# Modulation pieces and the first half's y moved inside a selective scan, and the norm, router and base matmuls after it taken by halves

## The reference

```python
mod = (_silu(L0_c) @ L0_wmod).reshape(1, 6, 1, -1)        # sa, ca, ga, sb, cb, gb; the same again with L1_wmod
h = _layernorm(x) * (1 + ca) + sa
# scan: xp = h @ x_proj_w.T -> dt_in, B, C;  dt = softplus(dt_in @ dt_proj_w.T + b)
#   state = exp(dt * A) * state + dt * B * h     per token, 512 channels x 16 states
#   y = sum over states of state * C  + D * h
x = x + ga * y
h = _layernorm(x) * (1 + cb) + sb
# base_out = h @ base_W.T + b;  logits = h @ router_W.T;  softmax, top 8 of 15, expert weights w
# lora = ((h @ A) * w) @ B * 2
x = x + gb * (base_out + lora)
# layer 1: modulation, layer norm, attention, modulation, layer norm, feed-forward
```

## Time and profile before

| what | value |
|---|---|
| median of 3 runs | 991.18 us (986.23 to 992.69) |
| the profiled execution, time | 988.8 us |
| its span, first to last instruction | 987.0 us |
| PE busy | 877.2 us (89%) |
| DVE busy | 749.6 us (76%) |
| ACT busy | 439.2 us (45%) |
| POOL busy | 264.5 us (27%) |
| mean granted TensorE clock | 0.957 of full speed |

### The profile page before, as it was taken

The page is one execution under the profiler, slowest core; times in us unless marked ns, Lnnn a source line. Parts: engine busy times, 40 slices in busy tenths (PEclk is TensorE's granted clock), DMA queues, the critical chain, the costliest instruction groups (busy, mean ns, idle before and its releaser), DMA issues.

```text
span 987.0 us, 12212 instructions
## 1 busy us (share of the span) xinstructions
PE 877.2 (89%) x4378; PEld 423.7 (43%) x4384; DVE 749.6 (76%) x1191; ACT 439.2 (45%) x822; POOL 264.5 (27%) x213
## 2 busy tenths in 40 slices
PE   3678868887776899989999999999999999999996
PEld 3224424443224544434455555555444444444442
DVE  6579999888899565637887788787524699876776
ACT  1637575645552102110066666666752465533200
POOL 1027789887894300005000000000000144200000
PEclk8769899999997999997999999999999999999998
DMA  9100060300002202451022211220006000000001
GB/s 353 65 1 0 1 255 1 128 0 1 0 0 72 100 0 89 135 181 38 15 69 74 74 37 40 73 75 2 2 1 224 5 0 1 0 1 0 12 33 43
DMA packets 29382, 54.35 MB, mean 55 GB/s; under 512 B 8021, under 2 KB 14805, under 8 KB 28041
## 3 DMA queue, kind: packets, MB, share of 16 engines
q1 hardware_dynamic: 29320, 53.57, 16.2%
HBM read 44.96 MB, written 8.39 MB: 54 GB/s over the span
## 4 chain that ended last, share of the span: by engine, by line
PE 58%; DVE 5%; SPq 3%; issue 3%; ACT 1%; DMA 0%; POOL 0%; DVEq 0%; POOLq 0%
PE ps L1075 15%; PE ps L940 8%; PE ps L922 6%; PE ps L1086 6%; PE ps L904 4%; PE ps L909 3%; PE ps L996 3%; PE ps L976 3%; SPq L302 2%; PE ps L857 2%; PE ps L962 2%; PE ps L925 1%; PE ps L907 1%; PE ps L851 1%; PE ps L725 1%
## 5 line engine op out<-in xcount | busy, mean ns | idle before, releaser
L678 ACT ACTIVATE prob<-ps 128x512 f32<-128x512 f32 x288 | 161.8, 599 | 138.6 <-PE ps L925 105.9
L458 POOL TENSOR_TENSOR hC<-hs,C_sb 128x512 f32<-128x512 f32 x128 | 163.0, 1284 | 70.1 <-DVE hs L1240 59.5
L832 PE MATMUL ps<-hC,identf 128*128 128x512 f32 x256 | 137.1, 644 | 35.6 <-POOL hC L458 33.5
L1354 DVE TENSOR_REDUCE mrow<-ps 128x4 f32<-128x512 f32 x160 | 103.7, 687 | 24.1 <-PE ps L907 15.8
L922 PE MATMUL ps<-stack 123*128 123x512 bf16 (+3 forms) x384 | 113.7, 327 | 0.2
L414 POOL TENSOR_TENSOR rstd<-veps,mhalf 128x4 f32<-128x4 f32 x8 | 8.4, 1052 | 381.4 <-DVE veps L1113 381.4
L612 ACT ACTIVATE ps<-dtT,nA 128x512 f32<-128x512 f32 x128 | 88.3, 691 | 42.2 <-DVE hs L1240 42.0
L1357 DVE TENSOR_REDUCE mrow<-ps 128x1 f32<-128x512 f32 x128 | 82.2, 685 | 25.1 <-PE ps L909 25.1
L832 PEld LDWEIGHTS ps<-hC,identf 128*128 128x128 f32 x256 | 45.3, 197 | 109.5 <-POOL hC L458 90.9
L1218 DVE TENSOR_TENSOR dBx<-uT,ps 128x512 f32<-128x512 f32 x112 | 74.9, 669 | 21.0 <-ACT B_sb L590 14.4
L940 PE MATMUL ps<-prob,V 128*32 128x512 f32 (+3 forms) x768 | 81.6, 498 | 0.7 <-ACT prob L678 0.7
(11 more groups left out here) (192 smaller groups left out, 1328.0 us busy)
## 6 DMA issues: line engine op xcount, KB each, us to landing
stack<-parts_dram SPq DMA_DIRECT2D x192, 64.0 KB
wmod<-in_wmod SPq DMA_DIRECT2D x4, 1536.0 KB, 11.2
parts_dram<-qkp SPq DMA_DIRECT2D x48, 128.0 KB, 1.8
wmod<-in_wmod SPq DMA_DIRECT2D x4, 1024.0 KB, 9.9
wattn<-in_wattn SPq DMA_DIRECT2D x1, 3072.0 KB, 10.3
wg<-in_wg SPq DMA_DIRECT2D x1, 2752.0 KB, 12.2
wu<-in_wu SPq DMA_DIRECT2D x1, 2752.0 KB, 9.5
wd<-in_wd SPq DMA_DIRECT2D x1, 2560.0 KB, 11.5
```

What stands on the lines that cost most here:

```text
L458: pool.tensor_tensor(hC[:, c, :], hs[:, c, :], C_sb[:, m % 2, :], ALU.mult).then_inc(S["hc_done"], 1)
L678: A_(prob[:, u % 4, j, :], ps[:, 3 + F % 3, :], ACT.Exp).then_inc(S["exp_done"], 1)
L832: mm(ps[:, c, :], identf[:], hC[:, c, :], start=False, stop=(s == NS - 1), skip_group_check=True).then_inc(S["sum_done"], 1)
L1354: v.reduce_max(mrow[:, kb, :, i], ps[:, bank, :].rearrange("p (j c) -> p j c", c=P), AX) \
```

## The change

1. **Pieces inside the step.** From step 16 on a piece stands on PE after the second of the step's four sums (`c == 2`) and no longer ahead of `broadcast(m + 1)`. ACT's copy of it goes to the next step. The piece now waits for C's copy of the next step (`c_evac` at `m + 2`).
2. **Rows in halves.** The 512-column rows are cut in two pieces of 256 columns: steps 7 and 8 for layer 0, 21 to 24 for layer 1. The column pieces of layer 1 stand in steps 12 to 15 and 17 to 20. SP's load of layer 1's wmod follows the piece of step 8.
3. **The first half's y.** The sixteen turning matmuls and the copies to uT leave step 16; `y_start` waits only for ACT's copy of the bank (`ym`). Four new pieces of kind "y" in steps 25 to 28 put a token tile of x into C_BANK by a matmul with the identity, add the four turned chunks on top, and ACT copies the sum to x_tok. The four DVE additions after the scan are gone.
4. **Halves after the scan.** DVE norms the first four tiles before it adds y to the last four. PE turns the first four, makes their router product, turns the last four, makes base_out(0), and then the router product of the last four; base_out(4) stands between hw's transposes and `lora_out`. The PSUM banks are dealt anew by `AR_BANK` and `F0_BANK`. SP's bias loads wait for the last turn (`yt`), no longer for x (`x0`).

```diff
+        for i_ in range(6):
+            SLOTS[1 + i_] = ("cols", 0, 2 + i_ // 2, i_ % 2 * 2)
+        for i_ in range(2):
+            SLOTS[7 + i_] = ("row", 0, 5, i_)
+        for i_, m_ in enumerate((12, 13, 14, 15, 17, 18, 19, 20)):
+            SLOTS[m_] = ("cols", 1, (0, 1, 3, 4)[i_ // 2], i_ % 2 * 2)
+        for i_ in range(4):
+            SLOTS[21 + i_] = ("row", 1, (2, 5)[i_ // 2], i_ % 2)
+            SLOTS[25 + i_] = ("y", None, None, i_)
...
+        AR_BANK = (0, 1, 4, 5)
+        F0_BANK = (2, 3, 6, 7, 4, 5, 6, 7)
...
-            sp.wait_ge(S["x0"], NT)
+            sp.wait_ge(S["yt"], NT)
...
+                if kind == "y":
+                    act.wait_ge(S["yt"], part + 1)
+                    A_(x_tok[:, part, :], ps[:, C_BANK, :], ACT.Copy).then_inc(S["x0"], 1)
+                    return
...
-                    if m == NS and c >= 2:
-                        for t in (2 * c - 4, 2 * c - 3):
-                            act.wait_ge(S["yt"], t + 1)
-                            A_(uT[:, t, half(0)], ps[:, t, :], ACT.Copy).then_inc(S["yb"], 1)
-                    if c == 2 and m in SLOTS:
-                        modulation(m)
+                    if c == 2 and m < NS and m in SLOTS:
+                        slot_out(m)
+                    if c == 2 and m > NS and m - 1 in SLOTS and m - 1 >= NS:
+                        slot_out(m - 1)
...
+            def slot(m):
+                kind, layer, j, part = SLOTS[m]
+                pe.wait_ge(S["c_evac"], m + 1 if m < NS else m + 2)
+                if kind == "y":
+                    pe.wait_ge(S["ym"], DC)
+                    pe.wait_ge(S["dg"], 2 * DC)
+                    mm(ps[:, C_BANK, :], identf[:], x_tok[:, part, :], start=True, stop=False, skip_group_check=True)
+                    for c in range(DC):
+                        ins = mm(ps[:, C_BANK, c * P:(c + 1) * P], dtT[:, c, tile(part)], dgA[:, c, :], start=False,
+                                 stop=(c == DC - 1), skip_group_check=True)
+                    ins.then_inc(S["yt"], 1)
+                    return
...
                 if h:
-                    pe.wait_ge(S["yb"], c + 1)
+                    pe.wait_ge(S["ym"], c + 1)
                 mm(ps[:, c, :], dgD[:, c, :], hT[:, c, half(h)], start=True, stop=False, skip_group_check=True)
...
-                    if c == 0 and m in SLOTS:
-                        modulation(m)
+                    if c == 0 and m in SLOTS and m < NS or c == 2 and m in SLOTS and m >= NS:
+                        slot(m)
...
                     broadcast(NS + 1)
-                    pe.wait_ge(S["dg"], 2 * DC)
-                    for c in range(DC):
-                        turn(0, c)
                     for c in range(DC):
                         y_start(1, c)
...
+            ln_transpose(1, 0)
+            pe.wait_ge(S["in_lf"], 48)
+            router(0)
+            ln_transpose(1, 1)
+            base_out(0)
+            router(1)
+            for t in range(1, 4):
                 base_out(t)
             pe.wait_ge(S["hw_done"], 1)
             for t in range(NT):
                 pe.transpose(ps[:, t // 4, (t % 4) * P:(t % 4 + 1) * P], hw[:, t, :], identf[:]) \
                     .then_inc(S["hw_tr"], 1)
+            base_out(4)
             pe.wait_ge(S["hw_evac"], 2)
-            for t in range(4):
+            for t in range(5):
                 lora_out(t)
...
             for t in range(4):
-                v.wait_ge(S["yb"], t + 1)
-                tt(x_tok[:, t, :], x_tok[:, t, :], uT[:, t, half(0)], ALU.add).then_inc(S["x0"], 1)
-            for t in range(4):
                 v.wait_ge(S["x0"], t + 1)
                 ln_stats((t,))
             ln_var(0)
-            for t in range(4):
-                v.wait_ge(S["yt"], 4 + t + 1)
-                tt(x_tok[:, 4 + t, :], x_tok[:, 4 + t, :], ps[:, 4 + t, :], ALU.add).then_inc(S["x0"], 1)
+            ln_norm(1, 0)
+            for t in range(4, NT):
+                v.wait_ge(S["yt"], t + 1)
+                tt(x_tok[:, t, :], x_tok[:, t, :], ps[:, t, :], ALU.add).then_inc(S["x0"], 1)
             for t in range(4, NT):
                 v.wait_ge(S["x0"], t + 1)
                 ln_stats((t,))
             ln_var(1)
-            ln_norm(1, 0)
             ln_norm(1, 1)
```

More of the change, by code:

```diff
@@ L829, in _ @@
                         pe.wait_ge(S["c_evac"], N_ALL)
-                        turn(1, 0)
+                        turn(0)
                     pe.wait_ge(S["hc_done"], m * DC + c + 1)
@@ L867, in _ @@
                     .then_inc(S["hw_tr"], 1)
+            base_out(4)
             pe.wait_ge(S["hw_evac"], 2)
-            for t in range(4):
+            for t in range(5):
                 lora_out(t)
-            for t in range(4, NT):
-                pe.wait_ge(S["f0_y"], t - 3)
+            for t in range(5, NT):
+                if t >= 6:
+                    pe.wait_ge(S["f0_y"], t - 3)
                 base_out(t)
@@ L1336, in gated @@
                                 ln_norm(norm, 0)
-            gated("f0_mm", "f0_y", "x1", "x1pre", lambda t: 4 + t % 4, gb0, norm=2)
+            gated("f0_mm", "f0_y", "x1", "x1pre", lambda t: F0_BANK[t], gb0, norm=2)
             ln_norm(2, 1, (0, 2))
```

85 lines of the change are left out of this document (41 added, 44 removed).

## The result

The changed kernel takes 964.66 us (median of 4 runs, 961.34 to 965.73), the kernel before on the same chip 991.71 (4 runs, 986.23 to 992.69): the ratio is 0.973, 95% interval 0.969 to 0.976. The forecast was 963.5, the range 957 to 972. The profiled execution after took 964.11 us, its span is 962.3 (before 987.0) and its mean granted clock 0.968 (before 0.957). So the spans differ by 24.7 us, against 25.3 forecast. The medians differ by 27.1 us: the forecast was taken off the profiled execution of before, which lies 2.9 us under this median. The total agrees better than its parts.

The account below looks back on a forecast made before the run. DVE was taken to set the pace in the scan's second half, waiting 14.4 us for B_sb, with PE leading from about 350 us. 13.7 + 1.9 + 9.7 = 25.3 us off the profiled 988.8 gave 963.5, range 957 to 972.

Parts of the forecast that it names:

- The pieces behind two sums: Scan's second half: twelve pieces fit on PE between second and third sum, counted at nothing, 0.2 us at the tightest place.
- 0.7 us left at step 18: Scan, step 18: the broadcast comes about 1.2 us late against 0.5 us of slack, so 0.7 us of waiting stays.
- the sign that I had named: Scan's second half in the profile after: steps 17 to 28 longer than 6.7 us would show the prediction wrong.
- The second half's term, 13.7: Scan's second half: DVE's 14.4 us of waits for B_sb fall to 0.7, gaining 13.7 us; bounds 2.3 and 14.4.
- slower: Rival: PE at half clock in the scan's second half, twelve pieces at 3.12 us each, 1000.2 us; chance 0.02.
- The row of step 7, 1.9: Scan's first half: cutting the row removes DVE's waits of 1.08 + 0.82 us, gaining 1.9 us; bounds 0.9 and 1.9.
- After the scan, 9.7: Behind the scan: hw's transposes 9.0 us earlier plus 0.74 us of PE standing covered, 9.7 us; bounds 8.7 and 11.5.
- The upper bound of 11.5: Behind the scan: the largest gain, with the fast router value and the transposes at half their mean, 11.5 us.
- The port: After the scan: one DVE softmax-chain operation beside POOL's `pre_add` may take some 1.1 us longer; counted at nothing.
- The rival in which several operations pay: After the scan: every DVE operation meeting `pre_add` waits for POOL's current addition, 965.5 us; chance 0.07.
- Layer 1, counted at nothing: Layer 1, after the first QK matmul: no gain or loss of its own forecast, 0 us.
- The one in which the pieces aren't hidden: Scan's second half: each piece still costs the 0.95 us of a column piece, gain 13.9, 974.9 us; chance 0.08.

Follow-up runs that it names:

- run 4: The changed kernel with the second half's pieces back at the start of their step, on PE and ACT: 976.24 us, ratio 0.983.
- run 5: The changed kernel with the piece of step 15 moved to step 29, behind two sums: 961.10 us, ratio 0.968.
- run 9: The changed kernel measured once more without any edit: 964.50 us, ratio 0.972.
- run 1: The kernel before with only the pieces behind two sums and the rows in halves: 977.66 us, ratio 0.986.
- run 11: The changed kernel with layer 1's two rows as whole 512-column pieces in steps 21 and 23: 964.78 us, ratio 0.973.
- run 3: The changed kernel without the move of the first half's y (turns in step 16, DVE adds after the scan): 971.33 us, ratio 0.979.
- run 7: The changed kernel with base_out(0) ahead of the first router half and PSUM banks dealt to suit: 966.04 us, ratio 0.972.
- run 2: The kernel before with only the order by halves after the scan; DVE still adds the first half's y: 984.26 us, ratio 0.993.
- run 6: The changed kernel with POOL's eight bias-row additions (`pre_add`) started after hw: 967.88 us, ratio 0.975.

## Why the prediction was right, and where its parts were not

- **The pieces behind two sums: right.** "I count the twelve pieces at nothing." A step with a piece takes 6.49 us, and run 4 prices the other place at 11.6 us. The y piece, which had no row, takes PE 1.75 us (259.39 to 261.14); the estimate was 1.7 to 1.9. My 0.7 us left at step 18 measured 0.63. By the sign that I had named (steps 17 to 28 longer than 6.7 us) three steps fail, 17, 19 and 21, with 7.2, 7.5 and 7.5 us: the first holds that 0.63, the other two the slow sums. The nine others take 6.5.
- **The second half's term, 13.7, was too high by 2.9.** The waits fell by 14.39 - 3.54 = 10.85 us. 1.05 us of the difference is a wait that I did not look for: the prediction takes part 2 of the change at steps 7 and 8 alone, while the columns of layer 1 move to 12 to 15, and the copy of B by ACT begins with step 16's. The price of a piece at a step's start was in the earlier trace rows, 0.94; run 5 shows that the piece was the cause. The other 1.86 us are the two slow pairs of sums. The prediction read a clock of 1.00 over steps 16 to 25, not over the rest, where the clock of before was 0.92 (262 to 303 us), and took "slower" as a case for all steps or none; single steps at the lower level cost 0.93 each. In run 9 they don't occur, and before has one (0.75), so counting all 14.4 us but 0.7 as gained took that chance wait for one that the change removes. A slow pair in a step without a piece costs 0.73 to 0.77 us (before, runs 1, 4 and 11), with a piece 0.75 to 0.95 (after, runs 3, 7 and 11), so little of it is the piece's.
- **The row of step 7, 1.9: too high by 0.45, and by 0.79 more through chance.** The halves leave 0.45 us in place of 1.90, so 1.45 gained; "like the column pieces, beside which DVE did not wait" is the step that fails, and all twelve profiles with the halves have 0.42 to 0.45 there. The other 0.79 is the column piece at low clock ahead of them (3.41 us). In the profile of before a piece in the same stretch took 2.64 us (102.88, PE) at a clock of 0.69, and DVE did not wait; run 2 shows that the same first half can.
- **After the scan, 9.7: right, 10.1 measured.** The router's second half ended 25.6 us after the scan (25.9 forecast) and hw's transposes began 35.8 after it (36.2 forecast). Two errors cancel in it. I took the middle between 3.9 and 5.8 us for the first router half; it took the slow value, 5.82, behind 2.97 us of idle PE. And a half's transposes took 1.9 us, twice, where half of the earlier trace rows gave 2.6. The upper bound of 11.5 doesn't follow from its own terms: the fast value gives 10.7, and nothing there makes the missing 0.8.
- **The port: right as a mechanism and as a price.** One operation of the chain met `pre_add` and took 1.45 us in place of 0.28, 1.2 us longer (1.1 forecast), and it cost nothing, since PE was ready only at 327.5. How much of an addition the operation meets is chance: it took 0.39 us in run 9, the same code, and hw's transposes came 35.5 us after the scan there, as in run 6, which takes the meeting away. The rival in which several operations pay did not come, because `pre_add` was through at 319.26, before the next one at 319.77. Nor would every operation pay: the TENSOR_REDUCE at 317.64 stood beside the additions and took 0.28 us, as without them. Its rule holds for others where the meeting is long: in run 6 seven operations pay 0.95 us each, and POOL's eight additions take 12.25 us in place of 9.89. The Trainium skill, SBUF — State Buffer, section on SBUF's two separate sides, says that the instruction that starts first has the port pair for its whole length and blocks the other. An addition of POOL takes 1.23 us and the delays were 1.17 and, in run 9, 0.11, none longer than one addition, so the trace agrees.
- **Layer 1, counted at nothing: it gave 3.6 us**, and that made the sum come out. The code is the same. Windows of before and, under them in a fence of their own, of after:

```profile
383.00:393.00 10.00, 10.00 (x26) 4.84 (x25) 4.59 (x9) 3.96 (x6) 0.00 (x0) 0.83 0.41 133
...
423.00:433.00 10.00, 9.87 (x37) 4.79 (x37) 3.24 (x6) 1.00 (x2) 0.00 (x0) 0.83 0.58 164
```

```profile
361.50:371.50 10.00, 10.00 (x30) 4.87 (x29) 5.98 (x12) 4.16 (x6) 0.00 (x0) 1.00 0.50 170
...
401.50:411.50 10.00, 10.00 (x36) 4.61 (x35) 4.31 (x9) 1.38 (x2) 0.00 (x0) 1.00 0.52 151
```

Before has two stretches at a clock of 0.83 where after has 1.00, and its 128 QK matmuls take 59.4 us against 56.1 (the groups of both stages). The stage has the same code in all fourteen profiles and lasts between 63.8 and 67.4 us; in the two executions of the kernel after it is 63.8 and 65.8. So 2 us of it at least are chance. Whether the new order after the scan has a part in the rest is open: the two kernels with the old one have 67.4 and 67.3, of the twelve with the new one eight lie between 63.8 and 65.8, but runs 2, 4, 6 and 11 have 66.7 to 66.9. That the scan gave 3.6 us less than forecast and this stage 3.6 us more is luck.

Of the rivals none decided. The one in which the pieces aren't hidden (974.9) is what run 4 made, at 976.24.

## What to carry to other kernels

Work that borrows an engine inside a periodic loop is free in the gap in front of something that another engine makes late, and dear in front of the instruction that starts the next turn; find the gap in one quiet step's rows and cut the work to its size (1.75 us fitted here, 3.5 cost 0.9). When a table is dealt anew, price every entry that it displaces, above all at the seam between two halves of a loop. Once two engines end level (here DVE with hw and PE with base_out at 327.5 us), shortening one gives nothing: look at what comes after for both before you move a third engine's work. And before a list of waits is counted as a gain, look at each of them: one that stands behind slow matmuls at a low granted clock comes and goes by itself.
